# Two large loads moved from SP's queue to ScalarE's in a fused convolution, FFT-mixing and feed-forward kernel

## The chip, the cores and the metric

One core of one Trainium2 chip. The metric is the device time of one execution in microseconds (us); the number shown for a kernel is the median of its runs.

## What is computed

The input is x of 32 images, 96 channels, 56 x 56 pixels, float32. Cut to what matters:

```python
# layer 0: depthwise 7x7 convolution, layer norm over channels, two linear maps, residual
h = conv7x7_depthwise(x) + conv_b
h = gelu(layernorm(h) @ w1 + b1) @ w2 + b2
x = h * layer_scale + x
# layer 1, tokens: 3136 per image, 96 channels
t = tokens(x)
u = relu(bn1(layernorm(t) @ w1.T))                 # 192 channels
X = fft(u, axis=tokens)
y = ifft(relu(X.real*rd - X.imag*id + rb) + 1j*relu(X.imag*rd + X.real*id + ib)).real
t = t + bn2(y @ w2.T)
t = t + qlinear(relu(qlinear(layernorm(t), W1)), W2)  # fp8 e5m2 products
out = from_tokens(t)
```

## The kernel before

Two phases. `conv_phase` (some 620 us) does the convolution of all images and leaves the result in DRAM as `h_tokens`. `image_phase` does the rest, one image after the other, with three images under way at once: turn n works on part 1 of image n (the linear maps of layer 0, the residual, the first layer norm and the outer Fourier transform), part 2 of image n - 1 (the spectrum) and part 3 of image n - 2 (back transform and feed-forward), and prepares hn, the normalised transpose of h, for image n + 1. The turns are "start" (-1), "first" (0), "second" (1), 29 times "steady" in a loop, "last" (31), "after" (32) and "end" (33).

A turn is cut into chunks c of four token rows (7 chunks, or 8 for the spectrum). What an engine does in a turn is a list of (step, chunk) pairs. `STAGES` (lines 84 to 93) gives each step a due time on PE and a distance between chunks, `LATER` shifts it for each engine, and `stages` sorts. Each engine works its list in order; semaphores (`Signal`, with `at(n, c)` for "chunk c of turn n is done") tie the lists together. The steps that matter here:

- M1, M2: the two maps of layer 0 on PE (L989, L995). ScalarE evicts M1 with the gelu (L762); DVE evicts M2 and adds `x_sb`, the image's input (L859), into `t1`. SP stores t1 to `residual_stream` (L614).
- A: the outer transform on PE (L1017); ScalarE copies it to `outer` (L770); SP stores it to `outer_spectrum` in three DMAs per chunk (L637).
- After A c=6, SP waits for all these stores (L641 to L643) and loads `inner` from them in three DMAs (L647, L648): a small part of 336 KB for B c=0 and a large one of 2016 KB for the rest. They serve the next turn.
- B, W, IB: the spectrum part on PE (L1028, L1037, L1044). B c=0 waits for the small part of inner, B c=1 for the large (L1023). SP stores IB to `inner_inverse` (L656), waits for those stores (L659 to L661), and loads `back` (L666), which AP (L1051) of the next turn reads.
- AP adds `t_old`, fetched by SP (L599); S2, N2, T2, F1, G, F2 are layer norm and feed-forward; the output of the image is stored at the turn's end (L671).
- L0S, L0N, HT: statistics of h on DVE (L823), normalisation on POOL (L701), transposes on PE (L982), eviction to `hn` on ScalarE (L747). M1 c=0 of the next turn needs all of hn.

Two loads serve the next image. **h** (`h` from `h_tokens`, 112 partitions x 24 x 112 numbers, in runs of 448 bytes, L606) may overwrite h as soon as POOL has normalised the image before, signal `h_normed`. **x** (`x_sb` from `x`, 96 rows of 12.5 KB, L595) may overwrite x_sb when the last M2 of the turn is evicted, signal `t1_done`. Both are issued by SP: h at the very start of a turn's list, which comes behind the output store of the turn before, and x behind the residual store of M2 c=6.

Of the kernel before, what the change touches and what calls it, by code (L numbers as in the profile page):

```python
# [12 lines left out]
C = 96  # L13
# [5 lines left out]
NQ = NTOK // PT  # L19
CH = 4  # L20
NC = NQ // CH
# [4 lines left out]
CC = 4  # L26
# [398 lines left out]
def image_phase(nc, x_img, h_dram, t1_dram, g_dram, v_dram, wts, out_img):  # L425
# [8 lines left out]
    with ExitStack() as ctx:  # L434
        def sb(name, shape, dt=F32):
            return ctx.enter_context(nc.sbuf_tensor(name, shape, dt))
# [3 lines left out]
        def signal(name, per, unit=1, first=0):  # L440
            signals.append(Signal(ctx, nc, name, per, unit, first))
            return signals[-1]
# [8 lines left out]
        x_sb = sb("x_sb", [C, NTOK])  # L451
        inner = sb("inner", [PT, NS, H2])
        back = sb("back", [2 * K1 + 1, NQ, C])
        h = sb("h", [PT, NPART, NQ, CC])
# [30 lines left out]
        h_loaded = signal("h_loaded", 1, 16)  # L485
        x_loaded = signal("x_loaded", 1, 16)
# [14 lines left out]
        h_normed = signal("h_normed", NC)  # L501
# [5 lines left out]
        t1_done = signal("t1_done", NC)  # L507
# [81 lines left out]
        def _(sp):  # L589
            def turn(kind, n):  # L590
                p1, p2, p3 = (kind in k for k in (PART1, PART2, PART3))
                followed = kind in ("start", "first", "second", "steady")

                def load_x():
                    sp.dma_start(x_sb[0:C, :], x_img[bass.ds(n + 1, 1), :, :].rearrange("o c t -> (o c) t")  # L595
                                 ).then_inc(x_loaded.sem, 16)

                def fetch_t1(turn_, c):
                    sp.dma_start(t1_old[:, c % 3, :],  # L599
                                 t1_dram[bass.ds(turn_ - 2, 1), :, CW * c:CW * c + CW].rearrange("o c t -> (o c) t")  # L600
                                 ).then_inc(t1_fetched[c % 3].sem, 16)

                if followed:

                    sp.wait_ge(h_normed.sem, h_normed.at(n))
                    sp.dma_start(h[:, :, :, :].rearrange("p k q c -> p k (q c)"),  # L606
                                 h_dram[:, :, bass.ds((n + 1) * (NQ * CC), NQ * CC)].rearrange("k p f -> p k f")
                                 ).then_inc(h_loaded.sem, 16)
                if kind == "start":
                    load_x()  # L610
                for name, c in orders[kind]["sp"]:
                    if name == "M2":
                        sp.wait_ge(t1_done.sem, t1_done.at(n, c))
                        sp.dma_start(t1_dram[bass.ds(n, 1), :, CW * c:CW * c + CW].rearrange("o c t -> (o c) t"),  # L614
                                     t1[:, c % 4, :]).then_inc(t1_stored[c % 4].sem, 16)
                        if followed and c == NC - 1:
                            load_x()
                    if name == "FETCH":

                        sp.wait_ge(t2_done.sem, t2_done.at(n, c))  # L620
# [47 lines left out]
                if p3:  # L668
# [3 lines left out]
                                 ).then_inc(out_stored.sem, 16)  # L672

            turns(sp, turn)
            sp.wait_ge(out_stored.sem, out_stored.at(NB + 1))

# [57 lines left out]
        def _(act):  # L734
            def turn(kind, n):
                order, plan = orders[kind]["act"], plans[kind]

                def bank(name, c, m, w, parts, ring="act"):
                    return psum[0:parts, plan[(name, c, ring, m)][0], 0:w]

                for name, c in order:
                    if name == "HT":
                        act.wait_ge(ht_made.sem, ht_made.at(n + 1, c))
                        if c == 0:

                            act.wait_ge(m1_made.sem, m1_made.at(n))
                        nc.scalar.activation(hn_tiles(hn, c), turned_back(bank("HT", c, 0, CW, C)), ACT.Identity,  # L747
                                             bias=ln_gb[:, 1:2], scale=ln_gb[:, 0:1]).then_inc(hn_done.sem, 1)
                    if name == "IB":
                        act.wait_ge(unmix_made.sem, unmix_made.at(n, c))  # L750
                        w = chunk_pairs(c)
                        b, j = before(n, c, ND, 2)

                        act.wait_ge(unmixed_stored[c % 2].sem, unmixed_stored[c % 2].at(b, j // 2))
                        nc.scalar.copy(unmixed[:, c % 2, 0:w, :].rearrange("p s c -> p (s c)"),
                                       bank("IB", c, 0, w * C, PT)).then_inc(unmixed_done.sem, 1)
# [54 lines left out]
                    if name == "F2":  # L811
# [3 lines left out]
                        nc.scalar.copy(y16[:, c % 2, :], bank("F2", c, 0, CW, C)).then_inc(y16_done.sem, 1)  # L815

            turns(act, turn)

        @block.vector
# [299 lines left out]
def hn_tiles(hn, c):  # L1119

    tiles = hn[:, :].rearrange("c (q p) -> c q p", p=PT)[:, :, CH * PT // NQ * c:CH * PT // NQ * (c + 1)]
    return tiles.rearrange("c q (y e) -> c q y e", e=2)


def turned_back(bank):

    return bank[:, ::-1].rearrange("c (e y q) -> c q y e", e=2, q=NQ)
# [209 lines left out]
```

## Time and profile before

| | us |
|---|---|
| median of 3 runs | 4473.53 |
| lowest and highest | 4470.06, 4478.01 |
| the profiled execution, its time | 4475.72 |
| its span, first to last instruction | 4473.9 |
| PE busy | 4019.6 (90%) |
| DVE busy | 3309.6 (74%) |
| ScalarE busy | 2249.2 (50%) |
| POOL busy | 1835.7 (41%) |
| mean granted PE clock | 0.944 |
| queue of SP (q1), share of the 16 DMA engines | 42.5% |
| queue of ScalarE (q10), share | 1.8% |

Busy time is time in instructions that compute; issuing a DMA does not count. The granted clock is PE's clock as a fraction of its full level. A wait is put down to what released it. ScalarE's queue carries only the filters of the convolution phase.

### The profile page before, as it was taken

How to read it: one execution, taken by the hardware profiler on the slowest of the kernel's cores; microseconds unless marked ns; L12 is line 12 of the kernel's file. 1: busy time of each engine (PE TensorE's matmuls, PEld its weight loads, DVE VectorE, ACT ScalarE, POOL GpSimd, SP SyncE). 2: the span in 40 equal slices, each digit the busy share in tenths (PEclk: the TensorE clock that was granted, in tenths of full speed). 3: DMA queues.
4: the chain of work that ended last, by engine and by line, in shares of the span. 5: the costliest groups of instructions: out<-in, count | busy, mean ns of one | idle time of the engine just before them, and what ended most of it. 6: DMA issues, size and time to landing. Idle time of an engine off the chain costs nothing. (4 is left out here: it accounts for less than half of the span.)

```text
span 4473.9 us, 88338 instructions
## 1 busy us (share of the span) xinstructions
PE 4019.6 (90%) x22802; PEld 2880.1 (64%) x22802; DVE 3309.6 (74%) x10713; ACT 2249.2 (50%) x4610; POOL 1835.7 (41%) x2468
## 2 busy tenths in 40 slices
PE   5999959999999999999999999999999999999986
PEld 3444435667666666677677666767676666666664
DVE  2333335688888888888888888888888888888877
ACT  2433423455555555555555555555555555555543
POOL 1111163444444444444444444444444444444431
PEclk9999979999999999999999999999999999999996
DMA  6566633444444444444344444444444444444331
GB/s 173 154 174 178 167 93 90 114 116 119 116 119 118 119 120 119 111 109 108 110 111 110 114 111 109 120 119 119 118 118 118 118 120 119 114 119 116 109 98 54
DMA packets 420415, 532.47 MB, mean 119 GB/s; under 512 B 220047, under 2 KB 378493, under 8 KB 404413
## 3 DMA queue, kind: packets, MB, share of 16 engines
q1 hardware_dynamic: 405920, 510.40, 42.5%
q10 hardware_dynamic: 14272, 20.04, 1.8%
q14 instruction: 198, 1.62, 0.1%
q8 instruction: 25, 0.41, 0.0%
HBM read 295.18 MB, written 235.12 MB: 119 GB/s over the span
## 5 line engine op out<-in xcount | busy, mean ns | idle before, releaser
L684 POOL TENSOR_TENSOR scales<-sums,minus_half 112x4 f32<-112x4 f32 (+1 forms) x480 | 606.5, 1267 | 1783.8 <-DVE sums L839 1783.8
L726 POOL TENSOR_TENSOR both<-plus,minus 96x224 f32<-96x224 f32 (+1 forms) x1024 | 630.9, 641 | 348.6 <-DVE minus L898 297.5
L781 ACT ACTIVATE uw<-psum,spec 96x224 f32<-96x224 f32 (+1 forms) x1024 | 449.6, 512 | 412.2 <-PE psum L1028 410.1
L989 PE MATMUL psum<-hn,w_sb 96*128 96x448 f32 x1344 | 611.2, 595 | 32.2 <-ACT hn L747 32.2
L995 PE MATMUL psum<-hid,w_sb 128*96 128x448 f32 x1344 | 564.3, 557 | 2.1 <-ACT hid L762 2.0
L762 ACT ACTIVATE hid<-psum,b_sb 128x448 f32<-128x448 f32 x672 | 421.1, 634 | 280.8 <-PE psum L989 244.5
L1028 PE MATMUL psum<-inner_dft,inner 112*96 112x112 f32 x3712 | 432.2, 272 | 110.1 <-DMA inner<-outer_spectrum 110.0
L387 PE MATMUL c_psum<-c_xt,c_toeplitz 128*112 128x448 f32 x1152 | 477.3, 552 | 50.2 <-ACT c_xt L329 27.3
L415 DVE TENSOR_SCALAR c_h<-c_psum,c_bias 112x448 f32<-112x448 f32 x192 | 199.0, 1036 | 412.8 <-PE c_psum L387 412.8
L1028 PEld LDWEIGHTS psum<-inner_dft,inner 112*96 112x96 f32 x3712 | 406.1, 173 | 131.2 <-issue 117.7
L701 POOL TENSOR_SCALAR h_norm<-h,sums,scales 112x96 f32<-112x96 f32 x896 | 467.8, 539 | 0.3 <-POOL scales L684 0.2
L898 DVE SCALAR_TENSOR_TENSOR plus<-psum,spec,uw 96x224 f32<-96x224 f32 (+1 forms) x1024 | 425.5, 416 | 44.7 <-ACT uw L781 42.6
L1037 PEld LDWEIGHTS psum<-aw_sb,both 96*112 96x112 f32 x3712 | 399.3, 179 | 50.1 <-issue 28.4
L898 DVE SCALAR_TENSOR_TENSOR minus<-psum,spec,uw 96x224 f32<-96x224 f32 (+1 forms) x1024 | 424.9, 415 | 0.0
L989 PEld LDWEIGHTS psum<-hn,w_sb 96*128 96x128 f32 x1344 | 266.1, 208 | 238.3 <-issue 215.1
L1037 PE MATMUL psum<-aw_sb,both 96*112 96x96 f32 x3712 | 406.1, 262 | 2.1 <-POOL both L726 1.9
L1009 PE MATMUL psum<-aw_sb,t 96*112 96x192 f32 x1792 | 340.7, 330 | 40.2 <-DVE t L859 40.2
L995 PEld LDWEIGHTS psum<-hid,w_sb 128*96 128x96 f32 x1344 | 217.5, 171 | 210.1 <-issue 205.8
L790 ACT COPY mixed<-psum 112x384 f32<-112x384 f32 (+1 forms) x256 | 114.6, 448 | 471.8 <-PE psum L1037 471.8
L1009 PEld LDWEIGHTS psum<-aw_sb,t 96*112 96x112 f32 x1792 | 290.2, 177 | 82.9 <-DVE t L859 56.3
L925 DVE TENSOR_SCALAR xn<-t_rows,sums,scales 112x96 f32<-112x96 f32 x896 | 323.0, 421 | 23.5 <-POOL scales L684 23.5
L859 DVE SCALAR_TENSOR_TENSOR t<-psum,b_sb,x_sb 96x448 f32<-96x448 f32 x224 | 229.2, 1023 | 147.2 <-PE psum L995 131.4
(85 smaller groups left out, 6680.4 us busy)
## 6 DMA issues: line engine op xcount, KB each, us to landing
outer_spectrum<-outer SPq DMA_DIRECT2D x448, 168.0 KB
inner<-outer_spectrum SPq DMA_DIRECT2D x32, 2016.0 KB
c_xpad<-x SPq DMA_DIRECT2D x96, 392.0 KB, 11.3
h_tokens<-c_h SPq DMA_DIRECT2D x24, 1568.0 KB, 8.4
h<-h_tokens SPq DMA_DIRECT2D x32, 1176.0 KB, 14.0
x_sb<-x SPq DMA_DIRECT2D x32, 1176.0 KB, 7.6
residual_stream<-t SPq DMA_DIRECT2D x224, 168.0 KB, 2.0
inner_inverse<-unmixed SPq DMA_DIRECT2D x224, 168.0 KB, 2.3
```

Source lines behind the costliest of these rows:

```text
L387: last = pe.matmul(psum[0:PT, 4 + k % 4, 0:NB * NYB], toeplitz[:, c, half, BR * d:BR * (d + 1), :].rearrange("p t x -> p (t x)"), xt[:, sl ...
L684: nc.gpsimd.tensor_tensor(scales[which][:, at:at + w], su[:, :, 5], minus_half[:, 0:w], ALU.pow).then_inc(ready.sem, 1)
L701: last = nc.gpsimd.tensor_scalar(h_norm[:, c % 4, j, :].rearrange("p (k c) -> p k c", c=CC), h[:, :, q, :], sums[0][:, q, 3:4], scales[0][ ...
L726: last = nc.gpsimd.tensor_tensor(both[:, c % 2, m, 0:w, k * PT // 2:(k + 1) * PT // 2], half(plus), half(minus), ALU.subtract if k else AL ...
L762: nc.scalar.activation(hid[:, c % 2, m, :], bank("M1", c, m, CW, 128), ACT.Gelu, bias=b1_sb[:, m:m + 1]).then_inc(gelu_done.sem, 1)
L781: last = nc.scalar.activation(uw[:, j % 2, k, 0:w * PT // 2].rearrange("p (s k) -> p s k", s=w), re, ACT.Identity, bias=spec[:, m, shift:s ...
L898: last = nc.vector.scalar_tensor_tensor(out=dst[:, j % 2, k, 0:w * PT // 2].rearrange("p (s k) -> p s k", s=w), in0=im, scalar=spec[:, m, ...
L989: pe.matmul(bank("M1", c, m, CW, 128), w1_sb[:, m * 128:(m + 1) * 128], hn[:, c * CW:(c + 1) * CW], start=True, stop=True).then_inc(m1_mad ...
L995: last = pe.matmul(dst, w2_sb[:, m, :], hid[:, c % 2, m, :], start=(m == 0), stop=(m == KF - 1))
L1009: last = pe.matmul(dst[:, j * H2:(j + 1) * H2], t1[:, c % 4, at:at + PT], aw1_sb[:, :], start=True, stop=True)
L1028: last = pe.matmul(dst[:, s * PT:(s + 1) * PT], inner[:, CH * c + s, m * C:(m + 1) * C], inner_dft[:, :], start=True, stop=True)
L1037: last = pe.matmul(dst[:, s * C:(s + 1) * C], both[:, c % 2, m, s, :], aw2_sb[:, m, :], start=(m == 0), stop=(m == 1))
```

## The change

Both loads go from SP's list to ScalarE's. The load of h is issued as ScalarE opens a turn, after `h_normed`. The load of x is issued before ScalarE's first HT eviction of the turn, after `t1_done` of the last chunk. SP keeps everything else in the order it had.

```diff
--- before.py
+++ after.py
@@ -589,32 +589,16 @@
         def _(sp):
             def turn(kind, n):
                 p1, p2, p3 = (kind in k for k in (PART1, PART2, PART3))
-                followed = kind in ("start", "first", "second", "steady")
-
-                def load_x():
-                    sp.dma_start(x_sb[0:C, :], x_img[bass.ds(n + 1, 1), :, :].rearrange("o c t -> (o c) t")
-                                 ).then_inc(x_loaded.sem, 16)
-
                 def fetch_t1(turn_, c):
                     sp.dma_start(t1_old[:, c % 3, :],
                                  t1_dram[bass.ds(turn_ - 2, 1), :, CW * c:CW * c + CW].rearrange("o c t -> (o c) t")
                                  ).then_inc(t1_fetched[c % 3].sem, 16)
 
-                if followed:
-
-                    sp.wait_ge(h_normed.sem, h_normed.at(n))
-                    sp.dma_start(h[:, :, :, :].rearrange("p k q c -> p k (q c)"),
-                                 h_dram[:, :, bass.ds((n + 1) * (NQ * CC), NQ * CC)].rearrange("k p f -> p k f")
-                                 ).then_inc(h_loaded.sem, 16)
-                if kind == "start":
-                    load_x()
                 for name, c in orders[kind]["sp"]:
                     if name == "M2":
                         sp.wait_ge(t1_done.sem, t1_done.at(n, c))
                         sp.dma_start(t1_dram[bass.ds(n, 1), :, CW * c:CW * c + CW].rearrange("o c t -> (o c) t"),
                                      t1[:, c % 4, :]).then_inc(t1_stored[c % 4].sem, 16)
-                        if followed and c == NC - 1:
-                            load_x()
                     if name == "FETCH":
 
                         sp.wait_ge(t2_done.sem, t2_done.at(n, c))
@@ -735,11 +719,27 @@
             def turn(kind, n):
                 order, plan = orders[kind]["act"], plans[kind]
 
+                def load_x():
+                    act.dma_start(x_sb[:, :], x_img[bass.ds(n + 1, 1), :, :].rearrange("o c t -> (o c) t")
+                                  ).then_inc(x_loaded.sem, 16)
+
+                if kind in ("start", "first", "second", "steady"):
+
+                    act.wait_ge(h_normed.sem, h_normed.at(n))
+                    act.dma_start(h[:, :, :, :].rearrange("p k q c -> p k (q c)"),
+                                  h_dram[:, :, bass.ds((n + 1) * (NQ * CC), NQ * CC)].rearrange("k p f -> p k f")
+                                  ).then_inc(h_loaded.sem, 16)
+
                 def bank(name, c, m, w, parts, ring="act"):
                     return psum[0:parts, plan[(name, c, ring, m)][0], 0:w]
 
                 for name, c in order:
                     if name == "HT":
+                        if c == 0:
+
+                            if kind != "start":
+                                act.wait_ge(t1_done.sem, t1_done.at(n))
+                            load_x()
                         act.wait_ge(ht_made.sem, ht_made.at(n + 1, c))
                         if c == 0:
```

On ScalarE, in the list of the steady turn, these rows differ (before to after; L729 is the load of h, L723 that of x). The first piece is the opening of the turn:

```order
 L578 UNCONDITIONAL_BRANCH
 L578 ISA
+L729 ISA [waits h_normed]
+L729 DMA h<-h_tokens 112x24x112
+L759 ISA
 L761 ISA [waits m2_made]
 L762 ACTIVATE hid<-psum,b_sb 128x448 [waits m1_made]
```

The load of h now stands between the last HT eviction of the turn before and the first M1 eviction. The second piece is the first HT eviction, late in the turn:

```order
 L786 REGISTER_ALU
 L790 COPY mixed<-psum 112x96 [waits unmix_made,mix_made]
+L723 ISA [waits t1_done]
+L723 DMA x_sb<-x 96x3136
 L743 ISA
 L747 ACTIVATE hn<-psum,ln_gb 96x28x16 [waits m1_made,ht_made]
```

The load of x stands between the last W eviction and the first HT eviction. On SP, before the change, late in the steady turn (L595 is the load of x):

```order
L614 DMA residual_stream<-t 96x448
L595 ISA
L595 DMA x_sb<-x 96x3136
L634 REGISTER_ALU
L637 DMA outer_spectrum<-outer 56x768 [waits outer_done]
L637 DMA outer_spectrum<-outer 56x768
L637 DMA outer_spectrum<-outer 2x768
L654 REGISTER_ALU
L656 DMA inner_inverse<-unmixed 112x4x96 [waits unmixed_done]
```

After the change the two L595 rows are gone from it, and so are the two of L606 at the list's start.

## Rows read from the trace of the kernel before

**Rows 1.** The page's first block: engine, busy us (share of the span), instructions.

```profile
span 4473.9 us, 88338 instructions
...
PE 4019.6 (90%) x22802; PEld 2880.1 (64%) x22802; DVE 3309.6 (74%) x10713; ACT 2249.2 (50%) x4610; POOL 1835.7 (41%) x2468
```

**Rows 2.** L606, the load of h: count, ns min/median/max, first and last.

```profile
L606 SPq MOVE h<-h_tokens x29: 29/29/29, 845.2 to 4104.1; - x29
...
DMA to landing us min/median/max: 6.8/14.0/14.6
```

**Rows 3.** Waits from 800 to 4140 us: us in total, times, longest.

```profile
PE psum L1028 <- DMA inner<-outer_spectrum: 98.0, 31, 5.3
...
PE psum L982 <- POOL h_norm L701: 59.8, 49, 1.8
```

**Rows 4.** PE in order of time: start us, duration, what, count [idle before].

```profile
2352.34 2.50 PE L995 MATMUL psum<-hid,w_sb 128*96 128x448 f32 x6
...
2355.00 1.70 PE L1028 MATMUL psum<-inner_dft,inner 112*96 112x112 f32 x16
...
2363.32 1.84 PE L1028 MATMUL psum<-inner_dft,inner 112*96 112x112 f32 x16 [3.25 <-DMA inner<-outer_spectrum]
...
2366.34 3.40 PE L995 MATMUL psum<-hid,w_sb 128*96 128x448 f32 x6
```

**Rows 5.** SP's queue in order of time, 2300 to 2430 us.

```profile
2330.66 0.33 SPq L595 DMA_DIRECT2D x_sb<-x  x1
...
2336.19 0.70 SPq L656 DMA_DIRECT2D inner_inverse<-unmixed  x1
2340.95 0.64 SPq L666 DMA_DIRECT2D back<-inner_inverse  x2
...
2344.13 1.57 SPq L637 DMA_DIRECT2D outer_spectrum<-outer  x3
2350.69 0.87 SPq L647 DMA_DIRECT2D inner<-outer_spectrum  x2
...
2357.69 0.34 SPq L671 DMA_DIRECT2D out<-result  x1
2358.71 0.33 SPq L606 DMA_DIRECT2D h<-h_tokens  x1
```

**Rows 6.** ScalarE in order of time, 2326 to 2350 us.

```profile
2334.45 0.72 ACT L747 ACTIVATE hn<-psum,ln_gb 96x448 f32<-96x448 f32 x1
2335.93 0.24 ACT L755 COPY unmixed<-psum 112x96 f32<-112x96 f32 x1 [0.76 <-PE psum L1044]
...
2346.07 0.72 ACT L747 ACTIVATE hn<-psum,ln_gb 96x448 f32<-96x448 f32 x1 [0.86 <-PE psum L982]
2348.91 0.64 ACT L762 ACTIVATE hid<-psum,b_sb 128x448 f32<-128x448 f32 x1 [2.12 <-PE psum L989]
```

**Rows 7.** Stretches: length, busy us by engine, PEclk, share of DMA engines, GB/s.

```profile
2340.00:2342.00 2.00, 1.63 (x12) 1.32 (x10) 1.81 (x5) 2.00 (x5) 2.00 (x3) 1.00 0.20 32
...
2348.00:2350.00 2.00, 2.00 (x4) 0.92 (x3) 0.00 (x0) 0.64 (x1) 0.00 (x0) 0.50 0.57 223
2350.00:2352.00 2.00, 2.00 (x9) 1.16 (x8) 0.00 (x0) 0.98 (x2) 0.00 (x0) 0.69 0.15 15
...
2362.00:2364.00 2.00, 0.68 (x7) 0.69 (x8) 0.41 (x2) 0.00 (x0) 0.11 (x1) 1.00 1.16 380
...
2366.00:2368.00 2.00, 2.00 (x6) 1.06 (x5) 1.99 (x7) 1.08 (x3) 1.01 (x1) 0.50 1.13 240
```

**Rows 8.** DMA issues: what, count, KB each, median us from issue to landing.

```profile
x_sb<-x SPq DMA_DIRECT2D x32, 1176.0 KB, 7.6
...
out<-result SPq DMA_DIRECT2D x32, 1176.0 KB, 9.7
```

**Rows 9.** SP's queue in the last turn, 4280 to 4345 us.

```profile
4311.66 0.32 SPq L656 DMA_DIRECT2D inner_inverse<-unmixed  x1
4313.88 0.65 SPq L666 DMA_DIRECT2D back<-inner_inverse  x2
```

## Prediction

> **What bounds the kernel now.** I read the page's first block, then PE's waits over the steady turns, then one turn on PE, SP and ScalarE in order of time, and last the DMA engines' share in stretches of 2 us over the opening of that turn.
>
> PE is busy 90% of the span, DVE 74% [rows 1]. SP's MOVE for the convolution result h, once per steady turn, gives the turn's length: (4104.1 - 845.2) / 28 = 116.4 us [rows 2]. A microsecond of PE time lost or won in every turn is therefore worth one microsecond of the turn, times about 30 turns. Over 29 turns PE's longest named wait is for the transfer inner<-outer_spectrum: 98.0 us in 31 pieces, about 3.3 us per turn; the second is POOL's h_norm, 59.8 us or 2.1 us per turn [rows 3].
>
> In the turn that opens near 2346 us, PE does B c=0 at 2355.00, stands still for 3.25 us, and starts B c=1 at 2363.32, when the large part of inner has landed [rows 4]. The stall costs something behind it: the six L995 matmuls after it take 3.40 us, the same six before it 2.50, and in the stretch 2366 to 2368 the granted clock is 0.50, that is 1.2 of 2.4 GHz [rows 4, 7]. So this one transfer costs about 3.3 + 0.9 us per turn.
>
> What sets its landing is SP's list and the one queue under it [rows 5]. The store of inner_inverse c=7 is issued at 2336.19; the load of back, which waits for it, at 2340.95; the last outer_spectrum stores at 2344.13; the load of inner, which waits for those, at 2350.69; then out at 2357.69 and h at 2358.71. x went in at 2330.66, in front of all of it. While inner, out and h move, the DMA engines' share is over 1; at 2340 to 2342 it is 0.20 and at 2350 to 2352 0.15 [rows 7]. Both holes are SP waiting for one landing before it issues the next transfer.
>
> The Trainium skill, "DMA: Bandwidth & Descriptors", section "Issuing engines are not separate DMA queues", says that DMAs started by different engines end on the same 16 DMA engines, and that a second issuer saves only issue time. By that alone the sum would be nothing, since SP's two issues cost 0.33 us each; no run here tests it yet. I count it as the rival "same".
>
> **The change, part by part.**
>
> *Issue cost on ScalarE.* Two DMA issues per turn at 0.33 us each, the duration on SP, with a MOVE of 0.03 us [rows 2, 5]. At the opening ScalarE ends the last HT eviction at 2346.07 + 0.72 = 2346.79 and does nothing until 2348.91, when PE has made M1: 2.12 us of cover for 0.4 [rows 6]. At the first HT eviction it delays the piece of 2334.45 by 0.4 us; its next piece, at 2335.93, had waited 0.76 us for PE. So both are free; if the cover were gone, 0.4 to 0.8 us per turn. The waits added are past already: h_normed of the last chunk precedes the last HT, and t1_done of c=6 precedes SP's issue of x at 2330.66, while ScalarE comes to that place just before 2334.45 [rows 5, 6]. Behind them on ScalarE stand M1's and HT's evictions, so a late signal would hold PE; none is late.
>
> *Issue cost taken from SP.* 0.7 us per turn and one wait. SP is not late for itself; nothing gained, nothing lost.
>
> *x moves from 2330.66 to about 2334.4, and to a second queue.* It lands 7.6 us after its issue [rows 8], so near 2342 to 2344; M2 c=0 needs it at 2355. It no longer stands ahead of the inner_inverse store. With x ahead, SP waited 2340.95 - 2336.19 = 4.8 us from that store to the load of back; in the last turn, where no x is loaded, 4313.88 - 4311.66 = 2.2 us [rows 5, 9]. So back can be issued up to 2.5 us earlier. But the engines still have the same bytes. With some 1.5 us from issue to first data and 5.3 us of transfer, as h needs for the same size (below), x ends near 2341.3, and back, issued at 2338.4 at the earliest, begins near 2339.9; 1.4 us of x run beside it, and 2.5 - 1.4 leaves 1.1. From back's issue to inner's issue it is 9.7 us of queued transfer [rows 5]. I take inner's issue 0.9 us earlier, a little less, since x's row is long (12.5 KB) and back may wait behind it; bounds 2.5 earlier (all of the shorter wait kept) and 1 later (x's tail goes first, back does not move).
>
> *h moves from 2358.71 to about 2347, and to a second queue.* Before, it stood behind inner and out. out lands 2357.69 + 9.7 = 2367.4, h 2358.71 + 14.0 = 2372.7, so h alone needs 5.3 us of the engines, 1176 KB at some 227 GB/s [rows 2, 5, 8]. Nobody needs it early: DVE's statistics are due 25.5 us into the turn (35.5 in STAGES, less 10 in LATER). Now its data begins about 1.5 us after 2347, while the last outer_spectrum stores end. The engines' free share from 2348 to 2352 is 0.43 x 2 + 0.85 x 2 = 2.6 us [rows 7]; that much of h costs nothing. The other 2.7 us run inside the transfer of inner, which PE waits for.
>
> *Sum for inner's landing:* 5.3 (h) - 2.6 (the hole) - 0.9 (x out of the way) = 1.8 us later. PE's stall grows from 3.3 to 5.1 us. I pass this on whole: PE is busy nearly without a gap from there to the end of the turn, and the h_norm wait at the end hangs on a chain that PE itself starts. The next thing late is the fetch of t_old c=1, queued behind inner as before; it shifts with it. The low clock behind the stall costs 0.9 us already; a longer stall may add nothing or as much again, and I take nothing.
>
> 30 turns open with both loads: 30 x 1.8 = 54 us. The first openings (start, first) have no inner load beside h, and nothing is won or lost. The profiled execution took 4475.7 us for a span of 4473.9, 2.2 us above the median of 4473.53. The sum on the median: 4473.5 + 54 = **4528 us**.
>
> **The rivals.**
>
> *A. h goes wholly in front of inner* (slower still). The hole helps only if h's data flows before 2350; the h packets are small (448 B a run) and could keep the engines busy past the outer_spectrum stores, making inner's issue itself later. Price: 5.3 us x 30 = 159, with the clock's 0.9 x 30 = 27 at most 4660; around 4600 if half of the hole is lost. For it: shares above 1 while h and out move. Against: h is issued 4 us before inner.
>
> *B. Faster: the freed wait wins.* Mechanism: the inner_inverse store no longer lands behind x, so back, the outer_spectrum stores and inner start up to 2.5 us earlier, and h fits beside them. It decides when B c=1 starts less than 27.1 us after the last inner_inverse store (2363.32 - 2336.19). For it: the last turn's 2.2 us, and the stretch 2362 to 2364, where a store and a load run together at 380 GB/s, against 240 at 2366 to 2368, mostly h alone [rows 7], so two mixed queues may carry more than my sum allows. Against: h and inner are both loads. At 1.5 us earlier per turn 4473.5 - 45 = 4428; at the bound, 2.5 and the clock regained, 4372.
>
> *C. Same.* Gain from x and loss from h within 0.3 us of each other, or the engines serve SP's queue undisturbed: 4473.5. The skill's rule above lands here too.
>
> By the Trainium skill, same page, section "Queues, rings and completion order", each DMA engine takes turns between the queues that hold work, a packet at a time. By that h cannot block inner but takes its share until it is through, and inner's first part, which lands just before B c=0, would be late too; in my model that delay is inside the later stall and adds nothing.
>
> **How the numbers follow.** Forecast 0.52, A 0.13, B 0.25, C 0.10. 0.2% or 9 us is about what a measurement of this kernel can tell from no change; that is 0.3 us per turn. Faster 0.25, same 0.10, slower 0.65. The forecast's own range is 4485 to 4580. The range of 8 in 10 reaches to B's middle and into A: 4430 to 4605.
>
> **What would show it.** Right: in steady turns PE's wait before B c=1 is 4.5 to 6 us, its total for inner near 150 us; ScalarE's h issue about 12 us earlier than before; back issued 1 to 2.5 us sooner after the inner_inverse store; no new wait on ScalarE; the turn 118.2 us. Wrong: PE's wait for inner under 3 us, or inner's issue later though h has hardly begun, or a longer wait at M1 c=0, which would put the cost on ScalarE. If h runs only in the hole, B holds.

## The result and the profile after

The changed kernel took 4624.3 us (median of 4 runs, 4622.2 to 4625.4) against 4475.8 for the kernel before; the ratio is 1.0331, with a 95% interval of 1.0313 to 1.0349. It is slower by 148 us. The forecast had the sign, and 54 us; its range ended at 4605. In the second group of experiments below two executions of the kernel before were disturbed (5802 and 8144 us); they are left out of its median and of the ratios.

The page of the changed kernel, first block and DMA queues:

```profile
span 4623.6 us, 88367 instructions
...
PE 4074.6 (88%) x22802; PEld 2924.4 (63%) x22802; DVE 3310.3 (72%) x10713; ACT 2255.9 (49%) x4610; POOL 1844.1 (40%) x2468
...
q1 hardware_dynamic: 315808, 433.32, 34.6%
q10 hardware_dynamic: 104384, 97.12, 9.2%
```

As meant, 77 MB have moved from SP's queue (q1) to ScalarE's (q10). PE is busy 55 us longer than in [rows 1] with the same instructions, and the span is 150 us longer.

The line that loads h, now L729 on ScalarE's queue, answers to [rows 2]:

```profile
L729 ACTq MOVE h<-h_tokens x29: 29/29/29, 831.1 to 4234.6; - x29
...
DMA to landing us min/median/max: 6.8/11.3/14.8
```

The turn is (4234.6 - 831.1) / 28 = 121.55 us, against 116.39: 5.16 us more in each.

The waits of the steady turns (in total, times, longest) answer to [rows 3]:

```profile
PE psum L1028 <- DMA inner<-outer_spectrum: 177.5, 56, 5.7
```

These are the waits from 800 to 4290 us, since the steady turns end later now; in the same window the kernel before has 101.9 us in 33 pieces. PE now waits 177.5 us for inner, in 56 pieces. Here is one opening, PE in order of time, as in [rows 4]:

```profile
2427.46 3.30 PE L1028 MATMUL psum<-inner_dft,inner 112*96 112x112 f32 x16 [5.73 <-DMA inner<-outer_spectrum]
2430.55 3.40 PE L989 MATMUL psum<-hn,w_sb 96*128 96x448 f32 x6
...
2436.81 1.77 PE L1028 MATMUL psum<-inner_dft,inner 112*96 112x112 f32 x16 [1.76 <-DMA inner<-outer_spectrum]
...
2439.13 2.42 PE L995 MATMUL psum<-hid,w_sb 128*96 128x448 f32 x6
```

Before, B c=0 found its part of inner landed, and B c=1 waited 3.25 us. Now B c=0 waits 5.73 us and B c=1 another 1.76. SP's queue in the same opening, as in [rows 5]:

```profile
2403.76 0.32 SPq L640 DMA_DIRECT2D inner_inverse<-unmixed  x1
2409.50 0.64 SPq L650 DMA_DIRECT2D back<-inner_inverse  x2
...
2419.39 0.87 SPq L631 DMA_DIRECT2D inner<-outer_spectrum  x2
```

And ScalarE with its queue, as in [rows 6]:

```profile
2401.76 0.33 ACTq L723 DMA_DIRECT2D x_sb<-x  x1
2402.28 0.72 ACT L747 ACTIVATE hn<-psum,ln_gb 96x448 f32<-96x448 f32 x1 [0.42 <-PE psum L982]
...
2413.76 0.33 ACTq L729 DMA_DIRECT2D h<-h_tokens  x1
2415.23 0.63 ACT L762 ACTIVATE hid<-psum,b_sb 128x448 f32<-128x448 f32 x1 [1.28 <-PE psum L989]
```

x goes out at 2401.76 and h at 2413.76, and ScalarE's own work is not held by them: its eviction behind h still waited 1.28 us for PE. Two links of SP's chain can be read off. From the last inner_inverse store to the load of back it takes 5.74 us (2403.76 to 2409.50) against 4.76. From inner's issue to the start of B c=1 it takes 17.42 us (2419.39 to 2436.81) against 12.63. The link between, back's issue to inner's, is 9.89 against 9.74. Together B c=1 starts 0.98 + 0.15 + 4.79 = 5.92 us later behind that store. About one microsecond comes back: the low clock now falls on the work between B c=0 and B c=1 (M1 c=1 takes 3.40 us), which waits for inner anyway, and the L995 matmuls behind B c=1 take 2.42 us instead of 3.40. 5.92 less 0.98 is 4.94, of the 5.16 us by which the turn grew.

Last, what each queue moved around inner's issue at 2419.39: packets, MB, share of 16 engines. q10 carries h here, q1 inner and what is queued behind it. In the changed kernel, 2420 to 2422 us:

```profile
q10 hardware_dynamic: 880, 0.39, 112.2%
q1 hardware_dynamic: 37, 0.03, 6.6%
```

So h and inner hardly move together: h goes ahead of inner. In 2422 to 2424 q1 has 62.7%, and from 2424 on q1 is alone. The changed kernel from 2424 to 2428, and the kernel before from 2354 to 2358, both with inner alone:

```profile
q1 hardware_dynamic: 1132, 0.86, 111.1%
```

```profile
q1 hardware_dynamic: 1249, 0.96, 110.6%
```

That is 215 GB/s against 240, with no h beside it in either. Then q1 from inner's issue to the start of B c=1, in the changed kernel and in the kernel before:

```profile
q1 hardware_dynamic: 3535, 3.57, 89.0%
```

```profile
q1 hardware_dynamic: 3476, 2.99, 99.3%
```

inner itself is 2394 KB, 2.45 MB. In the changed kernel q1 moved 1.12 MB of what is queued behind inner (the fetches of t_old, out and a store) before the last of inner had landed; before, 0.54 MB. So part of the engines' time went to later transfers while inner was unfinished.

Of the 4.79 us by which inner's transfer is longer, an estimate from these shares: q1 has 13.3% in 2350 to 2352 and 93.4% in 2352 to 2354 before, and 6.6% and 62.7% in 2420 to 2424 after. At 111% once it is alone, its data flows fully some 1.4 us after inner's issue before, and 3.4 us after. About 2.0 us are thus h in front of inner; about 2.8 us are inner taking longer behind h. Why it does, no run shows. The clock follows from the wait:

```profile
2428.00:2430.00 2.00, 2.00 (x13) 2.00 (x13) 0.00 (x0) 0.61 (x2) 0.00 (x0) 0.50 1.12 222
```

While B c=0 runs, behind a wait of 5.73 us, the granted clock is 0.50 (the number before the last two), which is 1.2 of 2.4 GHz.

### The profile page after: what moved, and what is told of

It is laid out like the page before. It is cut to its first block, busy times and chain, and to the rows that moved or that the text cites. A ratio compares the mean times of both kernels' runs of the same rounds, so it can differ in the third digit from the quotient of the medians.

```text
span 4623.6 us, 88367 instructions
## 1 busy us (share of the span) xinstructions
PE 4074.6 (88%) x22802; PEld 2924.4 (63%) x22802; DVE 3310.3 (72%) x10713; ACT 2255.9 (49%) x4610; POOL 1844.1 (40%) x2468
## 4 chain that ended last, share of the span: by engine, by line
PE 28%; DVE 23%; DMA 18%; issue 9%; SPq 3%; POOL 2%; ACT 2%; DVEq 1%; POOLq 0%; ACTq 0%
DMA inner<-outer_spectrum 9%; PE psum L989 6%; DVE stats L823 4%; PE psum L1028 4%; DMA outer_spectrum<-outer 4%; PE psum L995 4%; DMA inner_inverse<-unmixed 4%; DVE minus L898 3%; PE psum L1009 3%; PE psum L1037 3%; DVE plus L898 2%; PE psum L1017 2%; DVE xn L925 2%; DVE t L859 2%; DVE h L932 2%
## 5 line engine op out<-in xcount | busy, mean ns | idle before, releaser
L710 POOL TENSOR_TENSOR both<-plus,minus 96x224 f32<-96x224 f32 (+1 forms) x1024 | 643.0, 651 | 494.9 <-DVE minus L898 437.5
L989 PE MATMUL psum<-hn,w_sb 96*128 96x448 f32 x1344 | 643.6, 622 | 32.2 <-ACT hn L747 32.2
L1028 PE MATMUL psum<-inner_dft,inner 112*96 112x112 f32 x3712 | 468.0, 286 | 191.9 <-DMA inner<-outer_spectrum 191.8
L1028 PEld LDWEIGHTS psum<-inner_dft,inner 112*96 112x96 f32 x3712 | 438.7, 184 | 218.1 <-issue 201.0
L995 PE MATMUL psum<-hid,w_sb 128*96 128x448 f32 x1344 | 556.4, 550 | 2.0 <-ACT hid L762 2.0
L989 PEld LDWEIGHTS psum<-hn,w_sb 96*128 96x128 f32 x1344 | 283.1, 222 | 252.7 <-issue 229.3
L925 DVE TENSOR_SCALAR xn<-t_rows,sums,scales 112x96 f32<-112x96 f32 x896 | 338.0, 438 | 23.2 <-POOL scales L668 23.2
L909 DVE TENSOR_TENSOR t<-psum,t_old 96x448 f32<-96x448 f32 x224 | 138.1, 616 | 288.9 <-PE psum L1051 222.3
L995 PEld LDWEIGHTS psum<-hid,w_sb 128*96 128x96 f32 x1344 | 215.1, 169 | 204.1 <-issue 200.9
```

The costliest lines, as they stand in the source:

```text
L710: last = nc.gpsimd.tensor_tensor(both[:, c % 2, m, 0:w, k * PT // 2:(k + 1) * PT // 2], half(plus), half(minus), ALU.subtract if k else AL ...
L925: last = nc.vector.tensor_scalar(xn2[:, c % 2, j, :], t2_rows[:, c % 2, j, :], sums[2][:, j, 3:4], scales[2][:, at:at + 1], ALU.subtract, ...
L989: pe.matmul(bank("M1", c, m, CW, 128), w1_sb[:, m * 128:(m + 1) * 128], hn[:, c * CW:(c + 1) * CW], start=True, stop=True).then_inc(m1_mad ...
L995: last = pe.matmul(dst, w2_sb[:, m, :], hid[:, c % 2, m, :], start=(m == 0), stop=(m == KF - 1))
L1028: last = pe.matmul(dst[:, s * PT:(s + 1) * PT], inner[:, CH * c + s, m * C:(m + 1) * C], inner_dft[:, :], start=True, stop=True)
```

## The experiments

Turn lengths below are worked out as above, from the first and last issue of h in the profiled execution, which need not be the median one. All times are medians; "before" was run beside each group on the same chip, 4474.3, 4476.4, 4481.8 and 4473.0 us in the order of the four groups.

**First group: which load, and does the issuer or the moment matter?**

*Only x on ScalarE's queue*, ahead of the first HT eviction as in the change.

```diff
-                        if followed and c == NC - 1:
-                            load_x()
+                        if c == 0:
+                            act.wait_ge(t1_done.sem, t1_done.at(n))
+                            load_x()
```

> Only the load of x goes to ScalarE's queue; h stays on SP. Theory M (the moment of h: its transfer runs beside that of inner, and who issues it does not matter): x alone costs at most the 1.0 us per turn by which the load of back was issued later after the last inner_inverse store (5.74 against 4.76 us), so 4475 to 4510 us. Theory X (x's move is a main part of the loss, by way of back and the outer_spectrum stores): 4550 or more. Theory Q (a second queue in use costs by itself): in between, also with no later issue of back.

Measured: 4531.6 us, ratio 1.0132 (1.0112 to 1.0152), 57 us slower; the profiled execution was the fastest of the four (4519.6), and its turn is 117.64 us, 1.25 more. SP's queue in it:

```profile
2360.01 0.32 SPq L652 DMA_DIRECT2D inner_inverse<-unmixed  x1
2365.75 0.64 SPq L662 DMA_DIRECT2D back<-inner_inverse  x2
...
2375.37 0.87 SPq L643 DMA_DIRECT2D inner<-outer_spectrum  x2
```

Back again goes out 5.74 us after the last inner_inverse store. The cost was larger than theory M allowed, and the prediction had a gain here.

*Only h on ScalarE's queue, as the turn opens* (`load_h` is SP's wait and DMA, issued by ScalarE).

```diff
-                if followed:
-                    sp.wait_ge(h_normed.sem, h_normed.at(n))
...
+                if kind in ("start", "first", "second", "steady"):
+                    load_h()
```

> Only the load of h goes to ScalarE's queue, as a turn opens; x stays on SP. Theory M: nearly the whole loss of 148 us, so 4590 to 4630 us, with two stalls of PE per turn, before B c=0 (some 5 us) and before B c=1 (some 2). Theory X: 4550 or less.

Measured: 4601.2 us, ratio 1.0282 (1.0265 to 1.0300), 127 us slower; turn 120.18, 3.79 more. PE at an opening, and the median landing times:

```profile
2415.43 2.59 PE L1031 MATMUL psum<-inner_dft,inner 112*96 112x112 f32 x16 [3.28 <-DMA inner<-outer_spectrum]
...
2424.77 1.77 PE L1031 MATMUL psum<-inner_dft,inner 112*96 112x112 f32 x16 [2.52 <-DMA inner<-outer_spectrum]
```

```profile
h<-h_tokens ACTq DMA_DIRECT2D x32, 1176.0 KB, 10.5
...
inner<-outer_spectrum SPq DMA_DIRECT2D x32, 336.0 KB, 7.8
```

h is the main part. By turn lengths the two loads add up: 1.25 + 3.79 = 5.04 of 5.16 us. By the medians they do not: 57 + 127 = 184 us, and the change lost 148. In both runs the profiled execution was the fastest of the four, so how the loss divides between x and h is known only roughly. The small part of inner takes 7.8 us to land, where it had 3.7.

*h on ScalarE's queue, but issued when B c=1 has been made.*

```diff
                             act.wait_ge(spec_made.sem, spec_made.at(n, j))
+                            if j == 3 and kind in ("second", "steady"):
+                                load_h()
```

> h on ScalarE's queue, but issued only when B c=1 has been made, that is when all of inner has landed; x on SP. Theory M: no transfer of h beside inner any more, PE waits for inner 3.3 us per turn as before, 4460 to 4485 us. Theory Q: a loss of some tens of us stays, since h still uses the second queue and ScalarE still issues it.

Measured: 4480.3 us, ratio 1.0011 (0.9997 to 1.0026), no difference. Its wait for inner:

```profile
PE psum L1033 <- DMA inner<-outer_spectrum: 104.5, 33, 5.8
```

The wait is that of 800 to 4290 us, 101.9 us in 33 pieces before. Same queue, same issuer, and with the moment the loss is gone. Theory Q falls for h.

*The same, but when B c=0 has been made* (`j == 1` in the diff above).

> h on ScalarE's queue, issued when B c=0 has been made, so the small part of inner has landed and the large one is half through; x on SP. Theory M: the stall before B c=0 is gone, the large part lands up to 5.3 us later, 30 turns x 3 to 5.3 us: 4560 to 4630 us. If only the small part's delay costs (theory S: PE catches up by B c=1): 4475 to 4500.

Measured: 4485.3 us, ratio 1.0019 (1.0006 to 1.0032), 11 us slower. Theory M's 4560 to 4630 did not come true; theory S's 4475 to 4500 did, but not its reason, since the large part is not late at all: h is issued 7.3 us after inner (2361.90 against 2354.60), and B c=1 starts 12.49 us after inner's issue, as before. The queues from 2361.9 to 2367 us, when B c=1 starts:

```profile
q1 hardware_dynamic: 1411, 1.36, 113.9%
```

There is no line for q10: not one packet of h moved until then. h waited for inner and for what SP had issued behind it (in 2367 to 2370 q10 has 6.2%, in 2370 to 2373 101.7%), and landed 14.8 us after its issue.

**Second group: the queue, the order, and what paces the turn.**

*h on SP's queue, issued early*, behind the last outer_spectrum stores and ahead of the wait for them.

```diff
                     if name == "A" and c == NC - 1:
+                        if followed and more:
+                            load_h(n + 1)
                         for s in outer_stored:
```

(The last steady turn is taken out of SP's loop, since no image follows it: `more` is false there.)

> h stays on SP's queue but is issued early, behind the last outer_spectrum stores and ahead of the wait for them, so ahead of inner in the same queue. Theory M (the moment): h's 5.3 us less the hole of 2.6 us stand in front of inner, 2.7 us per turn, 4540 to 4570 us. Theory Q (two queues taking turns cost extra): this loses clearly less than h on ScalarE's queue at nearly the same moment (4601), so under 4580. If the queue is indifferent: 4590 to 4610.

Measured: 4592.3 us, ratio 1.0256 (1.0236 to 1.0277). PE and the landing times:

```profile
2408.44 3.13 PE L1040 MATMUL psum<-inner_dft,inner 112*96 112x112 f32 x16 [2.99 <-DMA inner<-outer_spectrum]
...
2417.49 2.00 PE L1040 MATMUL psum<-inner_dft,inner 112*96 112x112 f32 x16 [2.25 <-DMA inner<-outer_spectrum]
```

```profile
inner<-outer_spectrum SPq DMA_DIRECT2D x32, 336.0 KB, 7.6
```

The same two stalls, the same late small part; 116 us lost, against 127 with h on ScalarE's queue. One queue or two makes little difference, and h in front costs more than 2.7 us per turn here too: what failed is the sum for h, not the queue. This agrees with the rule of the Trainium skill ("DMA: Bandwidth & Descriptors", "Issuing engines are not separate DMA queues") that DMAs end on the same engines whoever starts them.

*h on ScalarE's queue behind the M1 c=0 evictions*, 1.3 us after inner's issue.

```diff
                                                  bias=b1_sb[:, m:m + 1]).then_inc(gelu_done.sem, 1)
+                        if c == 0 and kind in ("second", "steady"):
+                            load_h()
```

> h on ScalarE's queue, issued behind the M1 c=0 evictions, so about 1.5 us after inner has been issued instead of 4.5 us before it. Theory M with engines that take turns: none of h runs in the hole, all 5.3 us or more lie beside inner, 4630 to 4670 us, worse than h at the opening. Theory F (what is issued first is served first, also across queues): inner is ahead, nothing is lost, 4475 to 4490.

Measured: 4583.6 us, ratio 1.0234 (1.0214 to 1.0254); turn 120.31, 3.92 more. PE at an opening:

```profile
2424.23 3.30 PE L1033 MATMUL psum<-inner_dft,inner 112*96 112x112 f32 x16 [7.39 <-DMA inner<-outer_spectrum]
```

Between the two forecasts. The small part lands in 3.7 us, B c=0 does not wait, and B c=1 waits 7.39 us here, 17.78 us after inner's issue. This opening is one of the longer ones: over the steady turns that distance runs from 14.4 to 18.7 us, 15.8 in the median, against 12.7 before. The two queues from 2414 to 2418 us:

```profile
q1 hardware_dynamic: 855, 0.66, 68.2%
q10 hardware_dynamic: 855, 0.38, 45.7%
```

Here they do take turns, packet for packet, which they did not when h was issued 5.6 us ahead of inner (the changed kernel) or 7.3 us behind it. One stall or two, most of the loss is there: 107 us, against 127 with h ahead of inner. The turn lengths are nearer to each other (3.92 and 3.79 us) only because the profiled execution was the slowest here and the fastest there. How much of the 20 us is the small part's delay, and how much the idle stretch is worth against it, this run does not separate.

*Back loaded behind the last outer_spectrum stores*, both loads on SP as before.

```diff
-                    if name == "IB" and c == ND - 1:
+                    if name == "IB" and c == ND - 1 and not p1:
                         load_back()
...
                     if name == "A" and c == NC - 1:
+                        if p2:
+                            load_back()
                         for s in outer_stored:
```

> The kernel before, with SP's load of back moved behind the last outer_spectrum stores and in front of the wait for them; both loads stay on SP. The stores land before back instead of behind it, and back's transfer fills the hole in which SP waits for their landing, so inner is issued some 3 us earlier and lands some 2 us earlier. Theory M (PE is paced by inner's landing): 2 us per turn less, 4400 to 4440 us, unless back, now landing near 2351.5, holds AP c=0. If inner's landing does not pace the turn: 4475.

Measured: 4472.1 us, ratio 0.9990 (0.9980 to 1.0000), no difference. Its waits (steady turns), and PE at an opening:

```profile
PEld psum L1055 <- DMA back<-inner_inverse: 57.8, 29, 5.4
...
PE psum L1032 <- DMA inner<-outer_spectrum: 24.6, 18, 2.7
...
PE psum L1055 <- DMA back<-inner_inverse: 21.3, 26, 4.6
```

```profile
2343.76 4.84 PE L993 MATMUL psum<-hn,w_sb 96*128 96x448 f32 x6 [1.03 <-ACT hn L751]
2349.59 1.81 PE L1055 MATMUL psum<-outer_inv,back 115*96 115x112 f32 x8 [0.98 <-DMA back<-inner_inverse]
2351.19 3.46 PE L999 MATMUL psum<-hid,w_sb 128*96 128x448 f32 x6
...
2359.99 1.77 PE L1032 MATMUL psum<-inner_dft,inner 112*96 112x112 f32 x16
```

inner lands in time for B c=1, and its wait falls from 98 to 25 us. But back is late for AP c=0, and PE, idle there, stays at the low clock: AP and the L995 matmuls take 1.81 and 3.46 us, where [rows 4] has 2.50 for the latter. B c=1 starts 16.23 us after M1 c=0, and before 2363.32 - 2347.02 = 16.30. One stall has taken the place of the other. A wait removed is worth only the time to the next thing that is late.

*x on SP's queue, at the moment at which ScalarE issues it*, ahead of the last inner_inverse store.

```diff
+                        if followed and c == ND - 1:
+                            load_x()
                         sp.wait_ge(unmixed_done.sem, unmixed_done.at(n, c))
```

> x stays on SP's queue but is issued where ScalarE issued it in time, behind the store of outer_spectrum ahead of the last inner_inverse store (some 3.7 us later than before). The last inner_inverse store then stands behind all of x: back is issued 7 to 8 us after it instead of 4.8 (5.7 with x on ScalarE's queue). By theory M this costs more than x on ScalarE's queue (4532): 4540 to 4580. If the loss of x alone came from the second queue: 4475 to 4500.

Measured: 4527.1 us, ratio 1.0109 (1.0089 to 1.0129). SP's queue:

```profile
2356.10 0.30 SPq L658 DMA_DIRECT2D inner_inverse<-unmixed  x1
2361.76 0.64 SPq L668 DMA_DIRECT2D back<-inner_inverse  x2
...
2371.58 1.00 SPq L647 DMA_DIRECT2D inner<-outer_spectrum  x2
```

As with x on ScalarE's queue: back 5.66 us after the store, and 51 us lost against 57. So for x too the queue hardly counts, and the later moment does. That the store would stand behind all of x, as I wrote, was wrong.

**Third group: a version of my own, and the change on top of it.**

*inner's large part in two DMAs.*

```diff
-                        for part, (first, end) in enumerate(((0, CH), (CH, NS - 1))):
+                        for part, (first, end) in enumerate(((0, CH), (CH, 3 * CH), (3 * CH, NS - 1))):
...
-                        if c < 2:
-                            pe.wait_ge(inner_loaded[c].sem, inner_loaded[c].at(n - 1))
+                        if c in (0, 1, 3):
+                            part = (0, 1, 1, 2)[c]
+                            pe.wait_ge(inner_loaded[part].sem, inner_loaded[part].at(n - 1))
```

> The kernel before, with the large part of inner loaded in two DMAs, each with its own semaphore: 8 pairs, for which B c=1 waits, and 16 pairs, for which B c=3 waits. Same bytes, same order, same queue. Theory M (the turn is paced by the landing on which B c=1 waits): the stall of 3.3 us goes, but the fetch of t_old c=1, queued behind all of inner, is late next for AP c=1 and S2 c=1 right behind; 1 to 2 us per turn, 4410 to 4450 us. Theory P (as the run with back moved showed, PE is paced by something else at the opening): 4465 to 4480.

Measured: 4464.8 us, ratio 0.9956 (0.9939 to 0.9973), 17 us faster, less than the 30 to 70 expected. PE has no wait for inner among its larger ones any more, but a new one (waits of the steady turns):

```profile
PE psum L1058 <- DVE t L909: 86.5, 28, 4.5
```

That is S2 c=1, which waits for AP's addition and so, as I read it, for the fetch of t_old behind inner; the next run bears that out. 86.5 us stand where 98 stood, in a profiled execution that was the slowest of the four (4473.4 us).

*The same, with the fetches of t_old c=1 and c=2 ahead of the last outer_spectrum stores.*

```diff
-           "FETCH": -8.0, "FETCH NEXT": 10.5},
+           "FETCH": -8.0, "FETCH NEXT": 7.0},
```

> As the run with inner split, and SP fetches t_old c=1 and c=2 ahead of the last outer_spectrum stores instead of behind inner. Theory M: now nothing at the opening waits for inner's second half, 3.3 us of stall and some 0.9 us of low clock per turn are gone, 4350 to 4400 us. Theory P: 4460 to 4480.

Measured: 4414.4 us, ratio 0.9847 (0.9830 to 0.9863), 67 us faster than before and 210 below the changed kernel; turn (4051.7 - 845.8) / 28 = 114.50. PE's longest waits now:

```profile
PE psum L982 <- POOL h_norm L701: 64.1, 57, 1.8
...
PE psum L1009 <- DVE t L859: 55.9, 57, 1.7
...
PE psum L1058 <- DVE t L909: 35.4, 29, 1.4
```

The two transfers that were late at the opening are gone from the list. It ended above the 4350 to 4400 I expected: 35 us of the wait for t_old remain, and M1 c=0 keeps its low clock. The early fetches without the split were not run.

*The changed kernel with the same split and early fetches.*

> The changed kernel (both loads on ScalarE's queue) with the same split and the same early fetches. Theory M: B c=0 still waits for its part, which lands 8 us after its issue beside h, about 5 us of stall, but B c=1 does not wait again; the time lies some 60 to 130 us above the same split without the change, 4430 to 4530. If the loss of the change is only in the second half of inner: within 20 us of the split without it.

Measured: 4579.0 us, ratio 1.0218 (1.0200 to 1.0235), 165 us above the same kernel without the change, beyond my 60 to 130. Its wait for inner:

```profile
PE psum L1028 <- DMA inner<-outer_spectrum: 136.6, 28, 6.2
```

That is 4.9 us per turn in 28 single waits, before B c=0, from 800 to 4100 us. Where nothing waits for inner's end any more, h still holds its beginning; the split does not shield from it, and the version that had been fast has more to lose.

**Fourth group: the two open terms.**

*h in two halves*, 12 of its 24 blocks as the turn opens and the rest when B c=1 has been made, both on ScalarE's queue.

```diff
+                if kind in ("start", "first", "second", "steady"):
+                    load_h(0)
...
+                            if j == 3 and kind in ("second", "steady"):
+                                load_h(1)
```

> h on ScalarE's queue in two halves: the first as the turn opens, the second when B c=1 has been made; x on SP. With none of h at the opening the time was 4480, with all of it 4601. My hole of 2.6 us should take the first half (2.65 us) whole: 4475 to 4495. If every microsecond of h at the opening costs the same, hole or not: 4530 to 4550.

Measured: 4524.7 us, ratio 1.0126 (1.0108 to 1.0144), 52 us slower. PE at an opening, where inner is issued at 2371.00:

```profile
2375.49 1.77 PE L1038 MATMUL psum<-inner_dft,inner 112*96 112x112 f32 x16 [0.57 <-DMA inner<-outer_spectrum]
...
2384.39 3.24 PE L1038 MATMUL psum<-inner_dft,inner 112*96 112x112 f32 x16 [3.76 <-DMA inner<-outer_spectrum]
```

B c=1 starts 13.39 us after inner's issue, 0.76 more than before, and inner is issued 10.13 us after back, 0.39 more: 1.15 us for half of h. All of h cost 4.73 + 0.22 = 4.95 us by the same two links (in the run with h alone: 2424.77 less 2407.41, and 9.96 us from back to inner). The first half costs 1.15 of its 2.65 us, the second 3.80, more than it takes alone. So of the first half some 1.5 us are hidden, not all 2.65, although nearly all of it moves before inner's data (q10 has 1271 packets, 0.56 of its 0.60 MB, from 2368 to 2371.5), and the second half costs more than its own length.

*x on SP's queue behind the last inner_inverse store*, later than in any run before.

```diff
                     if name == "IB" and c == ND - 1:
+                        if followed:
+                            load_x()
                         for s in unmixed_stored:
```

> x on SP's queue, issued right behind the last inner_inverse store, so later still than in the run that issued it just ahead of that store (4527). If x's loss comes by way of that store landing behind x, it goes: the store lands in some 2.3 us, back is issued 2 us sooner, and x's own transfer then lies in front of back; 4470 to 4500. If it is the later moment of x's transfer itself that costs, since it takes engine time from back and the outer_spectrum stores: 4530 to 4580.

Measured: 4510.6 us, ratio 1.0088 (1.0067 to 1.0109), 38 us slower. SP's queue:

```profile
2355.58 0.32 SPq L656 DMA_DIRECT2D inner_inverse<-unmixed  x1
...
2357.23 0.65 SPq L668 DMA_DIRECT2D back<-inner_inverse  x2
...
2370.80 0.86 SPq L647 DMA_DIRECT2D inner<-outer_spectrum  x2
```

The store now lands in 1.5 us, back goes out 1.65 us behind it, 3.1 us sooner than before. And it does not help: x then runs in front of back and the last stores, and inner is issued 15.2 us after the store (2355.58 to 2370.80). Before it was 14.5, with x ahead of that store 15.5 on SP's queue and 15.4 on ScalarE's. The wait on the store was not what paced it; the loss stays when that wait is gone, and x's later transfer is what the three runs have in common.

## Why the prediction was right and wrong

*The path was right, the place of the stall was not.* PE is paced at the opening by inner's landing, an early h makes it later, and most of the delay is passed on to the turn. Shown by the four moments of h on one queue: 4601, 4584, 4485 and 4480. But the forecast was one wait of 4.5 to 6 us before B c=1; measured were 5.73 us before B c=0 and 1.76 before B c=1.

*Issue costs were nothing*, as said. h at B c=1 carries them and the wait, and measures 1.0011. ScalarE's DMA issues take 0.33 us each (2401.76, 2413.76), under the cover named.

*x's term failed, in sign.* "I take inner's issue 0.9 us earlier": it was 0.98 + 0.15 later in the changed kernel. I had read the 4.8 us between the inner_inverse store and back as the cost of standing behind x, from the last turn's 2.2, and kept what x's tail left of it. But in the last turn x is absent altogether. x was issued 5.53 us ahead of the last inner_inverse store before, and 2.00 us ahead of it in the changed kernel (2401.76, 2403.76); the engines' share in the 2 us around the same point is 1.09 before (2334 to 2336) and 0.88 after (2402 to 2404), so an earlier stretch is used less. The bound "1 later" was the one that held; "x's tail goes first, back does not move" was its text, and back moved 0.98 us later.

*h's term was mis-sized.* "5.3 (h) - 2.6 (the hole)" made 2.7 us: what does not fit into the hole delays inner, and inner's own transfer stays as long as it was. With h alone B c=1 starts 4.95 us later by the landing, in the changed kernel 4.79 us later after inner's issue. The part ahead of inner was about 2.0 us (an estimate from the shares above), no more than forecast. What the sum left out is that inner then takes some 2.8 us longer, at 215 GB/s against 240, and with 1.12 MB of later transfers moved before its end against 0.54. Half of h, nearly all of it in the hole, still cost 1.15 us. Why inner takes longer behind h is not shown.

*The sum* was 1.8 us per turn and the turn grew by 5.16. By turn lengths 2.1 of the difference come from x's term (-0.9 against +1.25) and 1.1 from h's (2.7 against 3.79). Over 30 turns 5.16 us are 155 us, and 148 were measured.

*The small part of inner* would be late and "adds nothing": it landed after 8 us instead of 3.7. The run with h behind M1, where it lands in 3.7, loses 107 us against 127, so most of the loss does not hang on the small part in this kernel. With inner split, PE's wait for inner is there alone (136.6 us in 28 waits before B c=0).

*Passing the stall on whole* was not right in size: 5.92 us later at B c=1 made 5.16 us of turn, and 4.95 with h alone made 3.79, since the low clock partly falls on time in which PE would wait anyway. For less stall it was further off: moving back took 2.5 us of the wait for inner away and gained nothing, since a wait for back took its place, and taking all away by the split gained 0.4%, since a wait for t_old did.

*Rival A* was nearest, in price (159 us) and in its title, "h goes wholly in front of inner": 880 packets of h moved in the first stretch behind inner's issue and 37 of q1. Its way there was not the one I gave, since inner's issue was hardly later (0.15 us). *Rival B* was to decide when B c=1 starts less than 27.1 us after the last inner_inverse store: it was 33.05 in the changed kernel (2403.76 to 2436.81). Even with x behind the store and back 3.1 us sooner, the opening at 2355.58 has B c=1 at 2383.44, 27.86 us. *Rival C*, SP's queue undisturbed, fails by the same packets for an early h; it describes h issued 7.3 us behind inner. That the engines take turns between queues, so that "h cannot block inner", showed only where h was issued 1.3 us behind inner (855 packets each); issued ahead of it, h did hold it back.

What I said would show me wrong, "inner's issue later though h has hardly begun", did appear: inner's issue was 1.13 us later behind the store, 0.98 of it before h was issued.

*The range* ended 19 us short. With x at the bound I had written down, 1 us later, and h less a hole of 1.5 us, the sum is 4.8 us per turn, 4618. That this comes near is partly luck: inner's landing moved by 5.92 us, and the clock gave some back. I had treated the two terms as if they could not fail together.

## What to carry to other kernels

Moving a bulk load to another issuer changes when it runs, and here that was nearly all that counted: ask which transfer that something waits for it will run ahead of or beside, and count all of its engine time against that one. Here an idle stretch of the engines between two dependent transfers hid less than its length, and the transfer behind the moved load took longer itself. Where a consumer waits on a whole transfer and needs only its beginning first, split it and fetch the small things ahead of it; remove the next late thing too before judging, since here the first split alone gained 0.4% and both 1.5%.

## What the runs showed of the hardware that I had not expected

- Two large loads in two queues behaved in three ways, by when they were issued. h issued 5.6 us ahead of inner: 880 packets of h and 37 of inner's queue in 2420 to 2422. h issued 1.3 us behind inner: 855 packets each in 2414 to 2418. h issued 7.3 us behind inner, which SP had finished issuing at 2359.95: no packet of h until B c=1 had its data, in the opening shown (2361.9 to 2367). What decides between them, no run settles.
- Behind h, inner alone moved at 215 GB/s (2424 to 2428), and at 240 in the kernel before (2354 to 2358), at a share over 1 in both; and 1.12 MB of transfers queued behind it moved before its last part had landed, against 0.54.
- Whether the second load sits in the same queue or another made 11 us of some 120 for h (116 lost against 127) and 6 of some 55 for x (51 against 57).
- A PE that had waited for h_norm and then again for back stayed at the low clock from M1 through the second group of matmuls (4.84, 1.81 and 3.46 us in the run with back moved; in the kernel before 4.59 for M1, then 0.93 and 2.50), so the wait for back cost more than its own length.
